# The inflow of a Mamba scan waits for the product two units behind it, in place of three

## The reference, cut to what matters

```python
delta = softplus(dt @ dt_w.T + dt_b)
dA  = exp(einsum('bld,dn->bldn', delta, A))
dBu = einsum('bld,bln,bld->bldn', delta, Bm, xc)      # the "inflow"
h = dA_t * h + dBu_t                                  # for every token t
y = einsum('bdn,bn->bd', h, C_t)                      # the "product", summed over n
```

## Time and profile before

| | us |
|---|---|
| median of 3 runs | 851.82 (850.19 to 853.87) |
| profiled execution, its own time | 846.1 |
| its span, first to last instruction | 844.3 |
| units begin / last scan ends | 44.9 / 701.8 |

### The profile page before, as it was taken

The page is one execution under the profiler, slowest core; times in us unless marked ns, Lnnn a source line. Parts: engine busy times, 40 slices in busy tenths (PEclk is TensorE's granted clock), DMA queues, the critical chain, the costliest instruction groups (busy, mean ns, idle before and its releaser), DMA issues.

```text
span 844.3 us, 12617 instructions
## 1 busy us (share of the span) xinstructions
PE 649.8 (77%) x3545; PEld 465.3 (55%) x3545; DVE 739.2 (88%) x1145; ACT 506.5 (60%) x1091; POOL 581.2 (69%) x487
## 2 busy tenths in 40 slices
PE   4438688878778877887877876886876789888991
PEld 2124445545355536764566635873554457788990
DVE  1376998989999999999999999999999897686774
ACT  2545795876688577464846577555854775444440
POOL 1094675677977797689958896789846994456451
PEclk9659899989989898997989988897887899999995
DMA  6923233223323336542464336532424621123247
GB/s 175 263 104 103 87 113 113 82 84 97 116 69 107 106 102 182 158 145 99 130 174 140 109 96 203 148 110 94 133 91 128 171 61 33 39 65 83 65 129 231
DMA packets 80248, 99.94 MB, mean 118 GB/s; under 512 B 10215, under 2 KB 48051, under 8 KB 80163
## 3 DMA queue, kind: packets, MB, share of 16 engines
q1 hardware_dynamic: 75859, 90.21, 36.3%
q0 software_dynamic: 4320, 8.92, 3.0%
HBM read 87.56 MB, written 15.35 MB: 122 GB/s over the span
## 4 chain that ended last, share of the span: by engine, by line
DVE 37%; PE 34%; issue 17%; ACT 7%; DMA 2%; POOL 2%; DVEq 1%; SPq 0%; ACTq 0%; POOLq 0%
DVE state L1077 18%; PE work_front L1248 4%; PE y L1288 4%; DVE product L1087 4%; PE up L1399 2%; PE work_front L1254 2%; PE y L1284 2%; PE up L1410 2%; PE gate L1392 2%; DVE stats L1007 2%; ACT decay L941 1%; DVE silu_m L1213 1%; PE gate L1313 1%; DVE arena L1052 1%; PE work_side L1332 1%
## 5 line engine op out<-in xcount | busy, mean ns | idle before, releaser
L818 POOL TENSOR_TENSOR inflow<-du,b_wide 128x1024 f32<-128x1024 f32 x128 | 315.5, 2468 | 145.0 <-DVE product L1087 92.0
L1077 DVE TENSOR_TENSOR_SCAN state<-decay,carry,inflow 128x512 f32<-128x512 f32 x192 | 234.7, 1264 | 6.5 <-ACT decay L941 6.5
L1087 DVE TENSOR_TENSOR product<-state,c_wide 128x1024 f32<-128x1024 f32 (+1 forms) x93 | 139.1, 1495 | 4.4 <-PE y L1284 3.3
L941 ACT ACTIVATE decay<-arena,a_neg 128x512 f32<-128x512 f32 x128 | 86.6, 688 | 60.7 <-DVE state L1077 56.9
L1284 PE MATMUL y<-ident,product 128*128 128x128 f32 x664 | 106.4, 305 | 20.6 <-DVE product L1087 20.5
L1284 PEld LDWEIGHTS y<-ident,product 128*128 128x128 f32 x664 | 87.2, 158 | 62.5 <-issue 34.7
L848 POOL DMA_INDIRECT y_dram<-y_rows,x_rows x71 | 82.5, 1162 | 56.0 <-ACT y_rows L997 49.1
L941 ACT ACTIVATE decay<-delta_odd,a_neg 128x512 f32<-128x512 f32 x128 | 86.6, 689 | 56.3 <-DVE state L1077 56.1
L1288 PE MATMUL y<-h_rows,ident 128*128 128x512 f32 x180 | 100.9, 652 | 7.0 <-ACT h_rows L906 6.5
L842 POOL DMA_INDIRECT row_dram<-m_tok,place x64 | 74.4, 1163 | 24.3 <-issue 12.7
L1077 DVE TENSOR_TENSOR_SCAN state<-decay,inflow 128x512 f32<-128x512 f32 x64 | 74.5, 1203 | 6.1 <-ACT decay L941 3.6
(11 more groups left out here) (232 smaller groups left out, 1342.6 us busy)
## 6 DMA issues: line engine op xcount, KB each, us to landing
b_wide<-bc_dram SPq DMA_DIRECT2D x128, 256.0 KB, 3.3
c_wide<-bc_dram SPq DMA_DIRECT2D x93, 256.0 KB, 3.5
w_stage<-gate_up_dram SPq DMA_DIRECT2D x26, 344.0 KB, 4.2
x_rows<-row_dram SPq DMA_DIRECT2D x71, 65.0 KB, 1.9
arena<-gate_up_dram SPq DMA_DIRECT2D x8, 344.0 KB, 4.4
x_tok<-in_x SPq DMA_DIRECT2D x8, 256.0 KB, 5.8
out<-x_tok SPq DMA_DIRECT2D x8, 256.0 KB, 4.8
inflow<-y_dram SPq DMA_DIRECT2D x6, 256.0 KB, 4.4
```

Source lines behind the costliest of these rows:

```text
L818: e.tensor_tensor(inflow[:, key % 3], du[:, c % 2], b_wide[:, key % ROW_SLOTS:key % ROW_SLOTS + 1, :].to_broadcast([P, HALVES, CHUNK]), AL ...
L941: e.activation(decay_bank[h][:], delta[c % 2][:, h, :], ACT.Exp, scale=a_neg[:, h, n:n + 1]).then_inc(S["decay"], 1)
L1077: e.tensor_tensor_scan(state[:, key % STATE_SLOTS, h, :], decay_bank[h][:], inflow[:, key % 3, h, :], 0.0 if c % (SEQ // CHUNK) == 0 else ...
L1087: e.tensor_tensor(product[:, key % 2, :, :wide], state[:, key % STATE_SLOTS, :, :wide], c_wide[:, key % ROW_SLOTS:key % ROW_SLOTS + 1, :wi ...
```

## The change

One wait is changed. The inflow of unit key now waits for the product of unit key-2, or for its scan where key-2 has share 4. Slots, order, and all other waits stay. All of the diff:

```diff
@@ -810,11 +810,11 @@
                     c, n = UNITS[key]
                     e.wait_ge(S[f"d_b{key % ROW_SLOTS}"], 16 * (key // ROW_SLOTS + 1))
                     e.wait_ge(S["du"], c + 1)
-                    if key >= 3:
-                        if share[key - 3] < SUB:
-                            e.wait_ge(S["times_c"], products[key - 3])
+                    if key >= 2:
+                        if share[key - 2] < SUB:
+                            e.wait_ge(S["times_c"], products[key - 2])
                         else:
-                            e.wait_ge(S["scan"], HALVES * (key - 2))
+                            e.wait_ge(S["scan"], HALVES * (key - 1))
                     e.tensor_tensor(inflow[:, key % 3], du[:, c % 2], b_wide[:, key % ROW_SLOTS:key % ROW_SLOTS + 1, :].to_broadcast([P, HALVES, CHUNK]),
                                     ALU.mult).then_inc(S["inflow"], 1)
```

## The result

The changed kernel takes 892.24 us in the median of 4 runs (891.25 to 894.78), the kernel before beside it 852.51. The ratio is 1.0477, with a 95% interval of 1.0458 to 1.0497: 40 us slower. The forecast was 876 us, slower by 24; the range, 854 to 893, holds the time at its far end, and the outcome called likeliest, 865 to 892, just misses it. The profiled execution took 891.5 us, its span is 889.7.

A forecast was written before the change was run, and what follows sets the result against it. DVE, busy 88% of the span, was taken to bound the kernel, with POOL not full. The terms 15.6 + 9.8 - 4.5 + 3 gave +24 us: 870 on the profiled execution, 876 on the median; range 854 to 893.

The forecast's parts named there:

- A: rstd2 on POOL stands behind the later inflow, so DVE's shift2 waits 1.95 to 5.3 us a chunk: +15.6 us.
- The walk through chunk 5: Turn-by-turn forecast of inflows and products n=0 to shift2: shift2 waits 5.3 us and ends 1.3 us behind today.
- B: At n=10, without a product, inflow n=12 is released by the scans and meets series and small: +9.8 us.
- C: Products n=0 to 4 lose less to inflows, -1.5 us in each of chunks 4 to 6: -4.5 us.
- D: DVE routing steps at n=13 to 15, in chunks without products there, meet inflows released by a scan: +3 us.
- Rival 3: Scans wait for inflows where POOL's turn, 6.5 us, exceeds DVE's: +51, 903 us; sign: over 15 us waited; chance 0.11.
- Rival 1: Inflows fall beside scans nearly everywhere, products and picked lose no lock time: some -37 at full, 833 with half; chance 0.11.

The follow-up runs named there:

- the runs with the early root: rstd2 made at end of turn n=3: changed kernel 890.4 us; same with old wait for inflows n=11, 12 881.7 us; kernel before 853.5 us.
- The copy: The kernel before, word for word, run again as an experiment: 850.4 us, ratio 0.9982.
- the three looser or earlier ones: Kernel before with four slots, inflow released by scan key-4: 911.5 us; four slots, product key-4: 884.3 us; three slots, scan key-3: 869.2 us.
- the hold in the light turns alone: Kernel before with the stricter wait only on the inflows of n=13, 14, 15 and 0: 875.4 us, ratio 1.0275.

## Why the prediction was right or wrong

The sign was right, and the stalls stood where the prediction put them. The size was 16 us short, and the sum's form was wrong: a stall's length proved not to be its price, since one taken away came back elsewhere. In DVE's row over the units the forecast had +24, measured were +38.0; head and tail gave another 7.4 of the span's 45.4, forecast at nothing.

- **A, what is queued behind the inflow.** Forecast +15.6. Measured +17.9 over the units: the shifts' waits for a root grew by 30.5 us, their own time fell by 12.6. The walk through chunk 5 forecast a wait of 5.3 us and a block of 4.1 ahead of it; the rows show 5.34 and 4.0. Chunks 4 to 6 waited as walked; in chunks 2 and 3 the wait was 4.0 and 4.2, in 1 and 7 it was 1.5. As a price of its own the wait fails all the same, by the runs with the early root.
- **B, small.** Forecast +9.8, measured +9.8. Its account, that the loss comes of inflow n=12 being released by the scans of n=10, was wrong: with the old rule for these inflows small kept its loss. Inflow n=11 behind product n=9, and n=12 right behind it, is what small meets. That the size agrees is in part luck.
- **C, products and scans.** This is the step that failed. Forecast was -4.5: products a little better, scans not felt. Measured: products +0.5, scans waiting for an inflow +7.3, so +7.8, 12 us off. The waits that are new stand in three places: 2.2 us in chunk 4, and 2.4 at scan n=5 of chunks 5 and 6. The walk ended at shift2 (n=5), 1.3 us behind, and took it that POOL had then paid. It was wrong on both sides of that point. From the start of the scans of n=1 to the end of shift2 chunk 5 took 28.4 us before (460.35 to 488.72) and 32.1 after (483.29 to 515.35), so 3.7 behind. One reason is in POOL's rows: the walk let POOL's `add` take the 1.0 us that it took in the kernel before, and behind inflow n=2 it took 1.97, while product n=1 ran:

```profile
486.83 1.97 POOL L848 DMA_INDIRECT y_dram<-y_rows,x_rows  x1 [0.17 <-issue]
```

Inflow n=3 so began later, right at product n=2, which lost 2.6 us and not 1.1; and inflow n=5 came behind product n=4, not ahead of it, and held the scan. Then it went on: by the scans of n=10 another 1.4 us were lost. The windows of chunk 5 from the scans of n=1 to those of n=10, before and after:

```profile
460.30:511.10 50.80, 42.53 (x221) 27.89 (x220) 49.51 (x56) 32.01 (x61) 45.58 (x45) 0.92 0.38 108
```

```profile
483.20:539.10 55.90, 41.59 (x215) 26.20 (x213) 47.61 (x56) 32.02 (x61) 49.94 (x49) 0.91 0.33 105
```

50.8 us before, 55.9 after, with DVE busy for less (47.6 for 49.5). POOL is busy for 45.6 of 50.8 us before: in this stretch it is nearly full, though its share of the span is 69%. An inflow that may begin only a turn later has little slack there to catch up from. Behind shift2 products n=7 and 8 lost 1.8 and 1.6 us that they had not lost before, and product n=6 won back 1.2.
- **D, the routing steps.** Forecast +3, measured +1.6 (both +4.3, picked -2.7).
- **Not in the sum:** w_stage +1.6, gate_h -3.5 and some 1.3 us of waits for PE and ACT; and the profiled run of before, which was a quick one. The copy's head and tail were longer by 3.3 us than that run's with the same instructions. The prediction set the profiled time against the median, but put the difference on both kernels as a constant: between the profiled spans lie 45.4 us, between the medians 39.7.
- **Rival 3** (much slower, 903) was nearer than the forecast, 11 us off for 16. It had the right view of POOL, that its turn with an inflow and its block exceeds DVE's; its threshold of 15 us of waiting scans was not reached (9.8), since shift2 took most of the waiting. The runs with the early root show what it looks like otherwise: 24.5 and 28.3 us.
- **Rival 1** (alignment) took the Trainium skill, "SBUF — State Buffer", section "SBUF: two separate sides", as its ground: the ports are an exclusive lock. The rows shown agree: the 128x512 products that meet no inflow take 0.69 us, the scans 2.45 for two under any inflow, and a product that meets one takes up to 3.93. But to be aligned an inflow must begin right behind a product and POOL must be free then. The kernel before has that in the light turns; the change makes the heavy turns late.

What stays open is the exact shape of the optimum. The partial versions of the stricter wait, the three looser or earlier ones and the moves in the queue were all slower or equal, and none beat the kernel before. That DVE and POOL pay for a change of the lead on either side is shown; that the kernel before is the best point of its neighbourhood is only what these runs suggest. Nor is it shown why the hold in the light turns alone costs as much as 24 us, why the roots ahead of the inflow take back 22, or what lowers the granted clock with the early root.

## What to carry to other kernels

Where two engines pass work to each other under a lock, a wait between them can set a balance, as here: held longer, the reader stood idle; held shorter, the two met in the lock. Read which of the two is paid (idle time or lengthened busy time) before moving the wait, and expect that one stall removed may come back at the next hand-over, as the early root showed. After such an edit read all waits again, those for the other engines too: half of what came back in the first of these runs was not POOL's. A sum of separate places came out too low here, where the supplying engine is nearly full in the stretch; look at that stretch's window (45.6 of 50.8 us), not at the share of the span (69%), and walk on until the lateness is paid back.

## What the runs showed of the hardware

- The lock reaches the smallest operations. A 128x4 DVE operation took 2.86 us in place of 0.16, a 128x3 copy 1.76 in place of 0.16: each was through only when the inflow was.
- Which row starts first doesn't tell who waits. Product n=2 of chunk 5 begins 0.32 us ahead of inflow n=3 (491.24 and 491.56) and ends 1.1 us behind it; the 128x4 operation began 0.46 us ahead of its inflow. In both, POOL's instruction before the inflow, an indirect DMA, was still running when DVE's row began.
- POOL waits too. Where inflows were released by a scan and met DVE operations with two operands in SBUF, their mean was 2.62 us (three slots) against 2.47, single ones took 3.2 us for 2.35. An `add` took 1.97 us for 1.01 while a product ran, and 2.01 in the kernel before.
- An additional buffer slot changed nothing (ratio 0.9998); a wait that lets it be used gave 1.0475.
